# Forty score tiles of the first heads placed between the products of the projection

## What is computed

```python
Q = (content @ Wq).reshape(b, n, HEADS, HEAD_DIM)      # K and V alike
scores = jnp.einsum('bqhd,bkhd->bhqk', Q, K) / math.sqrt(HEAD_DIM)
alpha = jax.nn.softmax(scores, axis=-1)
alpha = jnp.where(causal, alpha, jnp.zeros((), dtype=alpha.dtype))
Y = jnp.einsum('bhqk,bkhd->bqhd', alpha, V).reshape(b, n, d)
...
for e in range(E):
    h = jax.nn.gelu(flat_x @ w_fc[e], approximate=False)
    out = out + combine[:, e:e + 1] * (h @ w_proj[e])
...
x = L0_attn_content
x = x + _layernorm(_L0_attn_ref(_layernorm(x, axis=-1), L0_attn_Wq, L0_attn_Wk, L0_attn_Wv), axis=-1)
x = x + _layernorm(_L0_ffn_ref(_layernorm(x, axis=-1), L0_ffn_router_w, L0_ffn_w_fc, L0_ffn_w_proj), axis=-1)
```

## Time and profile before

| | us |
|---|---|
| median of three runs | 1622.24 (1619.61 to 1626.62) |
| profiled execution | 1626.82 |
| its span, first to last instruction | 1625.1 |

### The profile page before, as it was taken

The page is one execution under the profiler, slowest core; times in us unless marked ns, Lnnn a source line. Parts: engine busy times, 40 slices in busy tenths (PEclk is TensorE's granted clock), DMA queues, the critical chain, the costliest instruction groups (busy, mean ns, idle before and its releaser), DMA issues.

```text
span 1625.1 us, 31177 instructions
## 1 busy us (share of the span) xinstructions
PE 1455.0 (90%) x9750; PEld 836.1 (51%) x9751; DVE 1026.3 (63%) x1770; ACT 771.8 (47%) x1650; POOL 612.1 (38%) x711
## 2 busy tenths in 40 slices
PE   5988999999999899989999986389999999999990
PEld 3551233333333233323333243289999999999980
DVE  4769777777888788878888977723323233233324
ACT  2330577777777677767777785211111111111114
POOL 5332334543444334533444432123333333333332
PEclk9995899999999999999999998589999999999995
DMA  3569122022220222022213153262222222222229
GB/s 113 172 164 276 40 40 40 10 31 40 40 40 8 35 40 40 15 27 40 40 23 70 53 182 142 45 183 34 39 33 38 39 33 39 34 37 39 32 30 210
DMA packets 87629, 105.07 MB, mean 65 GB/s; under 512 B 11648, under 2 KB 70912, under 8 KB 87520
## 3 DMA queue, kind: packets, MB, share of 16 engines
q1 hardware_dynamic: 69664, 80.80, 21.5%
q0 software_dynamic: 17856, 22.89, 8.9%
HBM read 64.70 MB, written 38.96 MB: 64 GB/s over the span
## 4 chain that ended last, share of the span: by engine, by line
PE 61%; DVE 15%; issue 13%; ACT 4%; POOL 3%; DMA 2%; DVEq 1%; SPq 0%; POOLq 0%; ACTq 0%
PE ps L1153 16%; PE ps L1163 15%; PE ps L1008 10%; DVE negmax L1443 9%; PE ps L980 8%; PE ps L1094 8%; ACT wfc L868 2%; POOL x L668 2%; PE ps L973 2%; PE ps L1081 1%; DVE x L1348 1%; PE ps L1142 1%; ACT wfc L911 1%; DVE wfc L1454 1%; DMA arena<-in_L_ffn_w_proj 1%
## 5 line engine op out<-in xcount | busy, mean ns | idle before, releaser
L1443 DVE TENSOR_REDUCE negmax<-ps 128x1 f32<-128x1024 f32 x512 | 605.9, 1216 | 123.8 <-PE ps L1094 121.3
L868 ACT ACTIVATE wfc<-ps 128x512 f32<-128x512 f32 x768 | 436.6, 595 | 171.2 <-PE ps L980 162.7
L889 ACT ACTIVATE yx<-ps 128x512 f32<-128x512 f32 x142 | 84.8, 597 | 440.6 <-PE ps L1153 440.6
L1153 PE MATMUL ps<-yx 128*128 128x128 f32 x2272 | 270.3, 278 | 4.1 <-DMA arena<-in_L_ffn_w_proj 3.4
L1153 PEld LDWEIGHTS ps<-yx 128*128 128x128 f32 x2272 | 269.7, 195 | 8.3 <-DMA arena<-in_L_ffn_w_proj 3.6
L1163 PE MATMUL ps<-arena,yx 128*128 x1136 | 256.8, 379 | 0.0
L731 POOL TENSOR_TENSOR wfc<-wfc,causal 128x512 f32<-128x512 f32 x128 | 162.6, 1270 | 249.6 <-ACT wfc L868 181.7
L1094 PE MATMUL ps<-arena 96*128 96x512 bf16 x704 | 231.5, 413 | 9.6 <-DVE negmax L1443 4.0
L759 POOL DMA_INDIRECT expert_out<-yx,rt x71 | 112.6, 1586 | 318.3 <-DVE yx L1576 315.3
L1163 PEld LDWEIGHTS ps<-arena,yx 128*128 128x128 f32 x1136 | 210.4, 190 | 25.7
L980 PE MATMUL ps<-arena 120*128 120x512 bf16 x528 | 203.3, 392 | 12.8 <-ACT wfc L868 0.4
(11 more groups left out here) (177 smaller groups left out, 1364.7 us busy)
## 6 DMA issues: line engine op xcount, KB each, us to landing
arena<-qk_parts SPq DMA_DIRECT2D x132, 128.0 KB, 5.9
qk_parts<-x SPq DMA_DIRECT2D x32, 384.0 KB, 2.6
arena<-in_L_ffn_w_proj SPq DMA_DIRECT2D x8, 1024.0 KB, 8.6
wfc<-in_L_ffn_w_fc SPq DMA_DIRECT2D x16, 512.0 KB, 7.5
wfc<-qk_parts SPq DMA_DIRECT2D x60, 128.0 KB, 6.1
expert_out<-rt SPq DMA_DIRECT2D x3, 1408.0 KB, 12.0
yx<-in_L_attn_content SPq DMA_DIRECT2D x8, 512.0 KB, 3.9
x<-in_L_attn_content SPq DMA_DIRECT2D x1, 4096.0 KB, 25.5
```

Source lines behind the costliest of these rows:

```text
L868: nc.scalar.activation(et_sb[b % NET][:, hl, :], bk(ebank(c, g)), ACT.Exp).then_inc(s_expB, 1)
L889: nc.scalar.activation(hidT[s][:, 4 * hf:4 * hf + 4, :], bk(1 + hf).rearrange("p (c t) -> p c t", c=4), ACT.Gelu).then_inc(s_ge, 1)
L1153: ins = nc.tensor.matmul(bk(1 + hf)[:, c * P:(c + 1) * P], w1[s][:, kc * FF + (4 * hf + c) * P:kc * FF + (4 * hf + c + 1) * P], xsT[:, kc, :],
L1443: nc.vector.tensor_reduce(negmax[:, hl % 2, i:i + 1], ps[:, 2 * (k % 2):2 * (k % 2) + 2, :], AX.XY, ALU.max, negate=True).then_inc(s_max, 1)
```

## The change

**Projection with tiles.** Each chunk has eight positions. TensorE's order is: keys or queries 0, values 0, keys 1, values 1, transposes 0, transposes 1, keys 2, keys 3. From chunk 3 on, one unit of the attention follows in each position: 40 units, all 32 of group 0 and 8 of group 1; `groups` then begins at unit 8 of group 1. Queries and keys use banks 4 and 5, values and transposes banks 6 and 7, and tiles banks 0 to 3. All engines follow these positions in straight code. ScalarE takes over the normalisation (`apply_c`), both copies of the transposes and the second part (`part1`); VectorE keeps statistics, scale and shift (`bias_c`) and the remainder (`rest`). The maxima of group 0 are turned in bank 7.

**Loads and constants.** `load_group` 0, 1 and 2 stand behind the stores of chunks 1, 3 and 5. The rows of ones in the keys move from GpSimd to the head of VectorE's list. `ident` and the constant for ScalarE's table come first on GpSimd.

**Lists.** The one-hots lie in `yx` in place of the weights' arena, all in bf16, with the 16 rows of a batch innermost; a matmul of L1130 then reads them with a step of 16 elements. `iota_cn` is made by GpSimd. `place` waits for an earlier store. `store_x2(6)` and both `load_wproj` come ahead of the gates, and TensorE waits for `s_wp` ahead of the second product of tile 0.

```diff
-        hi1 = [arena[:, 4 * WSTEP + s * HW3:4 * WSTEP + (s + 1) * HW3].bitcast(BF16)
-               .rearrange("p (n v c) -> p n v c", v=3, c=NT) for s in range(HSL)]
+        yx_b = yx[:, :, :].rearrange("p t d -> p (t d)").bitcast(BF16)
+        LO1 = TOPK * TT * P
+        lo1 = yx_b[:, 0:LO1].rearrange("p (i j t l) -> p i j t l", i=TT // TPC, j=TOPK, l=P)
+        hi1 = [yx_b[:, LO1 + 2 * s * HW3:LO1 + 2 * (s + 1) * HW3].rearrange("p (v c n) -> p v c n", v=3, c=NT)
+               for s in range(HSL)]
+        iota_cn = yx_b[:, LO1 + 2 * HSL * HW3:LO1 + 2 * HSL * HW3 + NT * PCE].rearrange("p (c n) -> p c n", c=NT)
...
-        vtab = sb("vtab", [P, TOPK, TT])
+        vtab = sb("vtab", [P, TOPK, TT], BF16)
...
+        NC = NB * CPB
+        UNIT0, PER = 3, 8
+        PRO = PER * (NC - UNIT0)
+        def early(c, pos):
+            n = PER * (c - UNIT0) + pos
+            return [divmod(n, U)] if n >= 0 else []
+
         def groups(eng, body):
 
-            for p in range(2 * NSL):
+            body(1, 1, range(PRO - U, U))
...
+        def turn_bank(hl, g):
+            return 7 if isinstance(g, int) and g == 0 else 6 + HALVES[M_HALF[hl]]
...
+            def load_next(c):
+                sp.wait_ge(s_xt, KC * (c + 1))
+                sp.dma_start(xc[c % 2], x_t[:, (c + 2) * TPC:(c + 3) * TPC, :]).then_inc(s_x[c % 2], 16)
...
+            for c in range(NC):
+                if c + 2 < NC:
+                    load_next(c)
+                store_parts(c)
+                if c == CPB - 1:
+                    sp.wait_ge(s_ones, NSL)
                     for g in range(4):
                         sp.wait_ge(s_st[g], 16 * CPB)
-                    load_group(0, 0)
-            for u in range(1, NSL):
-                load_group(u, u)
+                if c >= CPB - 1 and (c - CPB + 1) % 2 == 0 and (c - CPB + 1) // 2 < NSL:
+                    load_group((c - CPB + 1) // 2, (c - CPB + 1) // 2)
...
+            store_x2(6)
+            for e in (4, 5):
+                load_wproj(e)
             for i in range(6):
                 store_gate(i)
-            for i in range(6, G):
-                store_x2(i)
+            store_x2(7)
             for i in range(6, G):
                 store_gate(i)
-            sp.wait_ge(s_inv, NPR // PCE)
-            for s in range(2):
-                sp.wait_ge(s_xs[s], 16)
-            for e in (4, 5):
-                load_wproj(e)
...
+            pool.memset(cst0[:, :], 0.0).then_inc(s_zero, 1)
             pool.memset(ident[:, :], 0.0).then_inc(s_const, 1)
+            pool.wait_ge(s_const, 1)
+            pool.affine_select(out=ident[:, :], in_=ident[:, :], compare_op=ALU.not_equal, fill=1.0,
+                               base=0, pattern=[[-1, P]], channel_multiplier=1).then_inc(s_ident, 1)
...
-            for u in range(NSL):
-                pool.memset(ks[u][MROW:MROW + MR], 1.0).then_inc(s_const, 1)
...
+            for c in range(NC):
+                for pos in range(PER):
+                    if pos == 0 and c:
+                        split(4 * c - 1)
+                    if pos in (3, 5):
+                        split(4 * c + pos // 2 - 1)
+                    for p, k in early(c, pos):
+                        body(p, p % NSL, (k,))
+                    if pos == 7:
+                        split(4 * c + 2)
+            split(4 * NC - 1)
...
+            pool.wait_ge(s_x2w[ORDER.index(G - 1)], 16)
+            pool.wait_ge(s_x2t, KC * (ORDER.index(G - 1) + 1))
+            pool.iota(iota_cn, [[P, NT], [0, PCE]], base=0, channel_multiplier=0,
+                      allow_small_or_imprecise_dtypes=True).then_inc(s_cn, 1)
...
+            def apply_c(n, s):
+                act.wait_ge(s_bias, n + 1)
+                for t in range(TPC):
+                    ins = nc.scalar.activation(xc[s][:, t, :], xc[s][:, t, :], ACT.Identity,
+                                               scale=rstd[:, s, t:t + 1], bias=negm[:, s, t:t + 1])
+                ins.then_inc(s_xn, 1)
+
+            def copy_xn(n, s, kc):
+                act.wait_ge(s_xt, KC * n + kc + 1)
+                wait_pos(act, s_qk, 4 * (n - 1))
+                nc.scalar.copy(xnT[s][:, kc, :], bk(6 + kc)).then_inc(s_xtc, 1)
+
+            def part0(n):
+                g = n % 4
+                act.wait_ge(s_qk, n + 1)
+                wait_pos(act, s_st[g], 16 * (n // 4))
+                nc.scalar.mul(parts[g][:, 0, :], bk(4 + g % 2), Q_SCALE if g < KC else 1.0).then_inc(s_p1, 1)
+
+            def part1(n):
+                act.wait_ge(s_res, n + 1)
+                nc.scalar.copy(parts[n % 4][:, 1, :], resid[n % 2]).then_inc(s_p2, 1)
...
+            root_c(0, 0)
+            apply_c(0, 0)
+            for kc in range(KC):
+                copy_xn(0, 0, kc)
+            root_c(1, 1)
+            for c in range(NC):
+                for pos in range(PER):
+                    if pos == 0:
+                        part0(4 * c)
+                    elif pos == 1:
+                        if c:
+                            part1(4 * c - 1)
+                        values(c, 0)
+                    elif pos == 2:
+                        part0(4 * c + 1)
+                        part1(4 * c)
+                        if c + 1 < NC:
+                            apply_c(c + 1, (c + 1) % 2)
+                    elif pos == 3:
+                        values(c, 1)
+                    elif pos == 4:
+                        if c + 1 < NC:
+                            copy_xn(c + 1, (c + 1) % 2, 0)
+                        part1(4 * c + 1)
+                    elif pos == 5:
+                        if c + 1 < NC:
+                            copy_xn(c + 1, (c + 1) % 2, 1)
+                    elif pos == 6:
+                        part0(4 * c + 2)
+                    else:
+                        if c + 2 < NC:
+                            root_c(c + 2, c % 2)
+                        part0(4 * c + 3)
+                        part1(4 * c + 2)
+                    for p, k in early(c, pos):
+                        body(p, p % NSL, (k,))
+            part1(4 * NC - 1)
...
+            def turn(n, s, kc):
                 pe.wait_ge(s_xn, n + 1)
+                wait_pos(pe, s_ve, 2 * (n - 1) + kc + 1 if n else 0)
+                if kc:
+                    wait_pos(pe, s_mtc, turned[0])
...
+            def keys(n):
+                c, g = divmod(n, 4)
+                if g == 0:
+                    pe.wait_ge(s_xtc, KC * (c + 1))
+                wait_pos(pe, s_res, n - 1)
...
+            for kc in range(KC):
+                turn(0, 0, kc)
+            pe.wait_ge(s_const, NCONST)
+            pe.wait_ge(s_ones, NSL)
+            for c in range(NC):
+                for pos in range(PER):
+                    if pos in (0, 2):
+                        keys(4 * c + pos // 2)
+                    elif pos in (1, 3):
+                        values(c, pos // 2)
+                    elif pos in (6, 7):
+                        keys(4 * c + pos - 4)
+                    elif c + 1 < NC:
+                        turn(c + 1, (c + 1) % 2, pos - 4)
+                    for p, k in early(c, pos):
+                        body(p, p % NSL, (k,))
+            pe.wait_ge(s_res, 4 * NC)
...
-                                           hi1[q % HSL][:, n, 0:2, :].rearrange("p v c -> p (v c)"),
+                    j, tt = divmod(q * PCE + n, TT)
+                    ins = nc.tensor.matmul(bk(7)[:, 0:2 * NT], lo1[:, ORDER.index(tt // TPC), j, tt % TPC, :],
...
+                if isinstance(t, int) and t == 0:
+                    pe.wait_ge(s_wp, 16 * E)
...
+                nc.vector.reciprocal(rstd[:, s, :], std[:, s, :]).then_inc(s_bn, 1)
+                dve.wait_ge(s_bn, CH * (n + 1))
+                nc.vector.scalar_tensor_tensor(out=negm[:, s, :], in0=mv[:, s, :, 0], scalar=-1.0, in1=rstd[:, s, :],
+                                               op0=ALU.mult, op1=ALU.mult).then_inc(s_bias, 1)
+
+            def rest(n):
+                g = n % 4
+                dve.wait_ge(s_p1, n + 1)
+                wait_pos(dve, s_p3, n - 1)
+                nc.vector.scalar_tensor_tensor(out=resid[g % 2], in0=bk(4 + g % 2),
+                                               scalar=Q_SCALE if g < KC else 1.0, in1=parts[g][:, 0, :],
+                                               op0=ALU.mult, op1=ALU.subtract).then_inc(s_res, 1)
...
-                dve.wait_ge(s_x2w[i], 16)
+                dve.wait_ge(s_x2w[i // 2], 16)
...
+            for u in range(NSL):
+                nc.vector.memset(ks[u][MROW:MROW + MR], 1.0).then_inc(s_ones, 1)
+            stats_c(0, 0, 16)
+            bias_c(0, 0)
+            stats_c(1, 1, 16)
             dve.wait_ge(s_const, NCONST)
+            for c in range(NC):
+                for pos in range(PER):
+                    if pos == 0:
+                        if c + 1 < NC:
+                            bias_c(c + 1, (c + 1) % 2)
+                        if c:
```

(31 more changed lines are left out.)

209 lines of the change are left out of this document (56 added, 153 removed).

## The result

The changed kernel takes 1634.3 us (median of 6 runs, 1631.8 to 1638.7), the kernel before 1621.95 in the same comparison (6 runs, 1619.6 to 1626.6). The ratio is **1.0067**, 95% interval 1.0055 to 1.0078: slower, by more than the 0.5% that the forecast set as its bound. The forecast was 1622 and "about the same"; the time lies in its range (1597 to 1640), inside rival (c)'s 1630 to 1638. In the later comparisons the kernel before had medians of 1624.6 (31 runs), 1625.1 (15) and 1624.6 (11), so that its first six runs lay some 2.6 low. The change was timed only beside those six: it costs 12.4 us in its own comparison and 9.7 against the later medians.

What follows compares the result with a forecast made beforehand. TensorE was taken to bound the projection, VectorE the 40 tiles alone after it. Front +8.5, clock -2.8 and lists -6.2 sum to -0.5 on 1626.82, less 4.6 above the median: 1622 us, range 1597 to 1640.

Steps and rivals of the forecast that it cites:

- rival (c): List matmul L1130: the step of 16 elements halves TensorE's reading or worse, 8 to 16 us more, 1630 to 1638; chance 0.14.
- The opening: Kernel start: three memsets of ones on VectorE at 3.5 us each, TensorE starting at 16.0, queries 0 at 18.7.
- Chunks: Projection: 13.4 us without tiles, 18.2 with tiles; chunks 2 and 4 take 25.1 and 25.3, held by inputs behind groups.
- rival (a): Chunks 2 and 4: the input is not held back behind a group; 1595, or 1608 for half, named 1600; chance 0.24.
- A restart: Projection: TensorE's first work after an idle stretch costs 3.1 us more, charged to chunks 0, 3 and 5.
- the front's total: Opening and projection with tiles, up to unit 40: start at 177.9 where it was 169.4, +8.5 us.
- The store behind group 2: Chunk 7: group 2 holds back the store of product 24, whose buffer is wanted there, costing 2 us.
- The clock's gain, -2.8: Attention's units 40 to 45: five steps at full clock take 7.35 us instead of 10.1, -2.8.
- The lists, -6.2: Between attention and experts: choice -2.7, one-hots and batches -2.6, weights' wait 0.9 less; sum -6.2 us.
- Rival (b): Ones quick on VectorE (-7 us), or chunks with tiles near TensorE's 15.2 (-2 each for five): 1613; chance 0.12.
- Rival (d): Chunks 3 to 7: TensorE's clock stays low, up to 12 us more a chunk, 1646 for two; chance 0.12.
- The base: Starting time of the sum: profiled execution of the kernel before, 1626.82 us, taken as 4.6 above the median.

Runs made afterwards that it cites:

- the experiment: Changed kernel with the inputs of chunks 4 and 6 issued ahead of groups 0 and 1 instead of behind them: 1619.78 us, ratio 0.9978.
- the mended kernels: Changed kernel with list reads at step 4, both inputs first, ones on GpSimd: 1603.52 us; with TensorE's zeroing wait one unit later: 1601.22 and 1604.39; stop filled: 1596.96.
- the kernel with the filled stop: Mended kernel with the zeroing wait one unit later, plus ten repeated matmuls of tile 40 filling TensorE's stop: 1596.96 us, ratio 0.9829.

## Why the forecast was wrong

Point by point, by its own steps.

- **The opening.** Forecast: ones from 0.8 at 3.5 each, transposes at 16.0. Measured: from 1.73 at 4.27 each, transposes at 18.71. The duration taken (3.5) is what the row shows as busy (3.47); the 0.80 between two memsets was missing. 1.6 of the 2.7 are this term, 0.9 the start. The Trainium skill (VectorE: DVE Perf Modes, section Zero memsets can be issued as uint32 (trn2)) gives one cycle per element, by which the forecast had worked out an estimate of 4.3 us each. The pitch of 4.27 agrees. The objection to it, that the row of 1024 elements was faster than that, compared a busy time with it, too.
- **Chunks.** Queries of chunks 0 to 7 start at 21.4, 36.4, 49.5, 74.7, 94.0, 119.5, 139.2 and 156.1, forecast 18.7, 35.2, 48.6, 73.7, 94.0, 119.3, 140.6, 157.8. No chunk's length is off by more than 1.6, though the start of chunk 0 is off by 2.7 and that of chunk 7 by 1.8. The 25.1 and 25.3 of chunks 2 and 4 are 25.2 and 25.5; rival (a), by which the input isn't held back, falls. A restart costs less than laid: chunk 5 takes 19.76 where 17.97 is the length without one (chunk 4 of the experiment), so 1.8 and not 3.1, and chunks 0 and 3 too were 1.5 and 1.0 shorter than laid; that made up for the opening, so that the front's total came out near by errors that cancel. Unit 40: 176.7, forecast 177.9.
- **The store behind group 2.** 2 us in chunk 7 were laid. The wait stands in ScalarE's timeline:

```profile
159.23 0.60 ACT L814 ACTIVATE x<-ps 128x512 bf16<-128x512 f32 x1 [2.33 <-DMA qk_parts<-x]
```

It reaches TensorE as the 2.02 for a head's parts, of which 0.82 stand in other chunks as well. So 1.2 us were on the path, and the 2 were too much.
- **The clock's gain, -2.8: did not come.** The sum took it that TensorE, warm from the projection, stays so. It came to unit 40 at full clock and was at 0.50 four microseconds later. The five steps from unit 40 to unit 45 took 9.75 us (176.66 to 186.41), where they had taken 10.16 (169.37 to 179.53 in the kernel before) and 7.35 were laid: 0.4 of the 2.8 came. Here the step was wrong, not its size: a TensorE that comes warm to the start of the attention loses its clock there. With it the front is +6.9 where +5.7 was forecast.
- **The lists, -6.2: the sign was wrong.** The choice came 2.2 earlier (4.7 late behind a front of 6.9) where 2.7 were laid, the one-hots took 0.70 to 0.75 as laid. The batches were laid at 2.0 and measured 4.15, which is 4 x 2.15 = 8.6 us, and -6.2 + 8.6 is +2.4, where the profiled executions have +2.1 (second tile: 9.0 late, of which 6.9 came from the front). This was rival (c), with a chance of 0.14, priced at +8 for a factor of two: its mechanism, place and price are those measured. Rival (b) fell with the ones at 4.27 and a chunk at 17.97. Rival (d), a low clock in chunks 3 to 7, came only for a few us behind each long stop: the clock read 0.50 from 74.5 to 79 and 0.92 from 79 to 84, and 0.50 from 119 to 124.
- **The base.** The forecast took the 4.6 us by which its profiled execution lay over the median of three runs off again; with more runs that median is 1624.6, so the base was right to 2.4 us. By the traces the terms should read -0.5 + 8.6 (the read) + 2.4 (the clock) - 1.2 (unit 40, earlier than laid) - 1.0 (the second tile's product) = +8.3, and the spans differ by 8.0.

Two terms of the sum failed, and both in the slow direction: the batch at 2.0 and the clock's gain. The first was a choice: between 2.0 and 4.1 a batch, with no row of such a read in the trace, the forecast took 2.0 since it was the row of the same line. That row was of another access pattern (contiguous), so it was no nearer to the new one than any other. At 4.15 the same sum gives 1630.6 from the forecast's 1622, and with 0.4 of the clock's gain in place of 2.8 it gives 1633.0; measured were 1634.3.

## What to carry to other kernels

Changing the layout of a tile changes the rate of everyone who reads it: a layout that makes VectorE's writes twice as fast (1.30 to 0.75) made TensorE's reads twice as slow, and a layout between the two (runs of four) kept the writes at 0.75 and cost the reads a tenth. That tenth is the price at the low clock, at which the contiguous reads ran; at full clock the same layout costs a factor of two. When a load is issued right behind a long group of transfers, count it as landing behind the group, and look for it in the row of the engine that consumes it, not in the row of the engine that stands; to issue the small urgent one first was worth 14.5 us here. And where an instruction is moved to another engine, take its distance from start to start, not the busy time of one.

## What the runs showed of the hardware

- TensorE's moving operand in bf16, 142 columns, 16 matmuls at the low clock: 2.0 us at a step of 2 bytes, 2.2 at 8, 4.1 at 16, 4.15 at 32. At full clock a single matmul falls from 0.12 to 0.065 us at 2 bytes and stays at 0.13 at 8.
- VectorE's one-hot of 128 x 1136, all operands bf16: 0.75 us with 4, 8 or 16 rows innermost, 1.34 with the 71 columns innermost.
- VectorE's memset of 4096 bf16 elements: 3.47 busy, 4.27 from start to start.
- An input of 512 KB issued behind twelve transfers of a group: 9.6 and 11.0 us from issue to use, 3.9 to 4.1 when alone.
- A group of twelve transfers of 128 KB, from its first issue to the first tile that uses it: 14.3, 13.9, 13.6, 11.2 and 10.8 us in five executions (the kernel with the input first, then four of the mended kernels). It varies by 3 us from one execution to another.
- In the kernel with the filled stop TensorE's clock fell to 0.50 behind a stretch in which it was busy for 2.96 of 5 us with no single stop over 1 us, after 5.00 of 5 at full clock.
